# A token-mixing and attention kernel: heads laid out on partition mod 32, bonus added ahead of the output transposes, one replicated v for a batch; GpSimd adds the pair term, queues reordered

## The reference, cut to what matters

```python
def step(s, rkvw):                      # s: (b, h, i, j), one state of 16x16 per head
    r_t, k_t, v_t, w_t = rkvw
    a = k_t[..., :, None] * v_t[..., None, :]
    out = jnp.einsum('bhi,bhij->bhj', r_t, u * a + s)
    s = a + w_t[..., :, None] * s
    return (s, out)
...
og = out.reshape(b, l, h, s_)
m = og.mean(-1, keepdims=True)
va = ((og - m) ** 2).mean(-1, keepdims=True)
og = ((og - m) / jnp.sqrt(va + 1e-05)).reshape(b, l, e) * gn_w + gn_b
x1 = x + og * g @ Wo.T
```

## Time and profile before

| | |
|---|---|
| median of 3 runs | 1774.38 us (1774.17 to 1774.59) |
| the profiled execution | 1773.87 us, span 1772.1 us, granted TensorE clock 0.991 |
| busy: TensorE / VectorE | 1728.8 us (98%) / 1636.2 us (92%) |
| busy: ScalarE / GpSimd | 1180.4 us (67%) / 935.7 us (53%) |
| DMA | 180.8 MB, 102 GB/s over the span |

### The profile page before, as it was taken

The page is one execution under the profiler, slowest core; times in us unless marked ns, Lnnn a source line. Parts: engine busy times, 40 slices in busy tenths (PEclk is TensorE's granted clock), DMA queues, the critical chain, the costliest instruction groups (busy, mean ns, idle before and its releaser), DMA issues.

```text
span 1772.1 us, 33090 instructions
## 1 busy us (share of the span) xinstructions
PE 1728.8 (98%) x11570; PEld 1234.0 (70%) x11570; DVE 1636.2 (92%) x2224; ACT 1180.4 (67%) x2952; POOL 935.7 (53%) x752
## 2 busy tenths in 40 slices
PE   8899999999999999999999999999999999999878
PEld 6667667677767677767767766767776777776646
DVE  3699999999999999999999999999999999999993
ACT  4665677676667676667767667767666777666543
POOL 1344556555655654655655555665465565555540
PEclk9999999999999999999999999999999999999989
DMA  6343343343333344334344433334333334433420
GB/s 257 82 102 105 93 105 94 99 120 97 100 103 99 91 114 106 104 91 104 93 104 115 102 92 107 94 95 120 100 99 101 98 94 110 101 93 94 104 84 13
DMA packets 81732, 180.82 MB, mean 102 GB/s; under 512 B 18304, under 2 KB 35072, under 8 KB 80544
## 3 DMA queue, kind: packets, MB, share of 16 engines
q1 hardware_dynamic: 59920, 161.93, 35.0%
q10 hardware_dynamic: 21648, 16.78, 3.1%
HBM read 161.91 MB, written 16.78 MB: 101 GB/s over the span
## 4 chain that ended last, share of the span: by engine, by line
PE 84%; DVE 10%; issue 3%; ACT 1%; POOL 1%; DMA 0%; SPq 0%; DVEq 0%; POOLq 0%; ACTq 0%
PE bank L2014 29%; PE bank L2021 17%; PE bank L2138 6%; PE bank L2059 5%; PE bank L2046 5%; PE bank L2026 5%; PE bank L2095 4%; PE bank L2033 3%; DVE S L873 2%; PE bank L2074 2%; DVE A L855 2%; DVE A L885 2%; PE bank L2116 1%; PE bank L2149 1%; PE bank L2039 1%
## 5 line engine op out<-in xcount | busy, mean ns | idle before, releaser
L855 DVE TENSOR_TENSOR A<-vrep,kt 128x1008 f32<-128x1008 f32 x256 | 311.3, 1225 | 2.5
L560 POOL COPY S<-s 128x16 f32<-128x16 f32 x128 | 81.7, 639 | 419.0 <-DVE A L885 418.8
L873 DVE TENSOR_TENSOR_SCAN S<-wrep,S 128x512 f32<-128x512 f32 x256 | 299.7, 1212 | 1.2 <-issue 0.2
L885 DVE TENSOR_TENSOR A<-S,rt 128x2048 f32<-128x2048 f32 x128 | 292.0, 2282 | 0.1
L534 POOL TENSOR_TENSOR xf<-xf,xa 128x512 f32<-128x512 f32 x160 | 223.1, 1396 | 39.2 <-DVE xf L811 39.1
L1496 ACT ACTIVATE bank<-bank,par 128x128 f32<-128x128 f32 x640 | 173.4, 366 | 39.9 <-PE bank L2095 39.3
L503 POOL TENSOR_TENSOR hrs<-hrs,mhalf 128x32 f32<-128x32 f32 x31 | 171.0, 5517 | 2.6
L552 POOL TENSOR_TENSOR rk<-rT,kT 128x256 f32<-128x256 f32 x32 | 105.9, 3311 | 103.7 <-DVE oc L910 103.7
L501 POOL TENSOR_SCALAR rstd<-mv 128x1 f32<-128x1 f32 (+1 forms) x96 | 73.8, 769 | 156.9 <-DVE mv L748 61.4
L863 DVE TENSOR_TENSOR S<-A 128x1008 f32<-128x1008 f32 x128 | 155.5, 1215 | 0.2
L811 DVE TENSOR_TENSOR xf<-bank,sx 128x512 f32<-128x512 f32 x160 | 108.2, 677 | 44.7 <-PE bank L2014 22.7
(11 more groups left out here) (165 smaller groups left out, 4093.1 us busy)
## 6 DMA issues: line engine op xcount, KB each, us to landing
vrep<-v_dram SPq DMA_DIRECT2D x256, 512.0 KB
xc<-x_c SPq DMA_DIRECT2D x32, 256.0 KB, 6.5
xs<-x_s SPq DMA_DIRECT2D x32, 256.0 KB, 7.2
v_dram<-vT ACTq DMA_DIRECT2D x32, 256.0 KB, 3.1
out<-rr ACTq DMA_DIRECT2D x31, 256.0 KB, 2.7
st<-state SPq DMA_DIRECT2D x64, 2.0 KB, 6.4
Wv<-big_w SPq DMA_DIRECT2D x1, 1024.0 KB, 7.3
Wk<-big_w SPq DMA_DIRECT2D x1, 1024.0 KB, 9.0
```

Of the source, the lines that this page charges most:

```text
L855: ve_.tensor_tensor(A[:, u % 2, half * WJ:(half + 1) * WJ, 0:P - 2], vrep[:, half, :, 0:P - 2], k, ALU.mult).then_inc(dve_outer.sem, 1)
L873: last = ve_.tensor_tensor_scan(s, w, s, 0.0, ALU.mult, ALU.add)
L885: ve_.tensor_tensor(out4, s, r, ALU.mult).then_inc(dve_read.sem, 1)
```

## The change

What lies on a partition changes for v, k, r, the decay, u and the initial state: channel i of head h, which was 16h + i, goes to chunk i mod 4 and partition 32 (i div 4) + h, that is, each chunk holds four of the 16 channels of all 32 heads, with the head on partition mod 32. The weights and parameters are permuted accordingly before the launch.

```diff
+    by_value = np.arange(E).reshape(H, HS // C, C).transpose(2, 1, 0).reshape(E)
+    u = a["L1_u"].reshape(E)[by_value]
...
+        "big_w": np.stack([chunked(a["L1_" + k].T[:, by_value] if k in ("Wv", "Wk", "Wr") else a["L1_" + k].T) for k in BIG]),
```

```diff
-            def load_vrep(n, p, v):
-
-                src = v_dram[p].rearrange("(c h j) t -> c h (j t)", c=C, h=HC)
-                u, half = v // 2, v % 2
+            def load_vrep(n, p, half):
+
+                src = v_dram[p].rearrange("(h j) t -> h (j t)", h=H)
                 v0 = held(sp, regs[0], 16 * (n + 1))
-                v1 = held(sp, regs[1], dve_outer.count(f"a{(v - 2) % V}", n if v >= 2 else n - 1))
+                v1 = held(sp, regs[1], dve_outer.count(f"a{V - 2 + half}", n - 1))
...
-                             src[u][:, half * WJ * P:(half + 1) * WJ * P].unsqueeze(1).broadcast_to([HC, HS, WJ * P]))\
-                    .then_inc(vrep_loaded[half], 16)
+                             src[:, half * WJ * P:(half + 1) * WJ * P].unsqueeze(0).broadcast_to([C, H, WJ * P])).then_inc(vrep_loaded[half], 16)
...
-                eng.dma_start(v_dram[p].rearrange("(c e) t -> e c t", c=C), vT[:, p, :, :]).then_inc(v_stored, 16)
+                eng.dma_start(v_dram[p].rearrange("(h g c) t -> g h (c t)", h=H, c=C), vT[:, p, :, :].rearrange("e c t -> e (c t)")).then_inc(v_stored, 16)
...
-                    eng.wait_ge(act_tail.sem, act_tail.count("o4", n - 1))
-                ones = slide[:, HC * (3 - u):HC * (7 - u)]
+                    eng.wait_ge(dve_sum.sem, dve_sum.count("o4", n - 1))
+                ones = head_rep[:, 0:H]
                 for g in range(4):
-                    last = pe.matmul(bank[SUM_BANK][32 * g:32 * g + 32, :], ones, A[:, u % 2, g:UJ:4, :],
+                    last = pe.matmul(bank[SUM_BANK][32 * g:32 * g + 32, :], ones, A[:, u % 2, C * g:C * g + C, :],
```

```diff
+                eng.wait_ge(pe_bonus.sem, pe_bonus.count("C", n - 1))
+                for c in range(C):
+                    sc.activation(rkc[:, c, 0:P], bank_of("Rp")[:, c * P:(c + 1) * P], ACT.Copy, scale=col("u", c))
                 sc.activation(rT[:, :, :], by_chunk(bank_of("Rp")[:, :]), ACT.Copy)
...
-                eng.wait_ge(pe_tail.sem, pe_tail.count("C", n - 1))
-                po.tensor_tensor(rku[:, :, :], rT[:, :, :], kT[:, :, :], ALU.mult).then_inc(pool_wkv.sem, 1)
+                po.tensor_tensor(rkc[:, :, 0:P], rkc[:, :, 0:P], kT[:, :, :], ALU.mult).then_inc(pool_wkv.sem, 1)
...
+            def wkv_rks(n, m, p):
+
+                eng.wait_ge(pool_wkv.sem, pool_wkv.count("rk", n))
+                eng.wait_ge(pool_rk2.sem, pool_rk2.count("rk2", n))
+                po.tensor_tensor(rkc[:, 0:2, :], rkc[:, 0:2, :], rkc[:, 2:4, :], ALU.add).then_inc(pool_rks.sem, 1)
+                eng.wait_ge(pool_rks.sem, pool_rks.count("half", n))
+                po.tensor_tensor(rkc[:, 0, :], rkc[:, 0, :], rkc[:, 1, :], ALU.add).then_inc(pool_rks.sem, 1)
...
-                for c in range(C):
-                    last = pe.matmul(bank_of("C")[:, c * P:(c + 1) * P], head_u[:, c, :], rku[:, c, :],
-                                     start=True, stop=True)
-                last.then_inc(pe_tail.sem, 1)
...
-                pe.matmul(bank_of("C2")[:, 0:C * T2], head_rep[:, :], rk2[:, :, :].rearrange("p c m -> p (c m)"),
-                          start=True, stop=True).then_inc(pe_tail.sem, 1)
+                pe.matmul(bank_of("C")[:, 0:P + T2], head_rep[:, :], rkc[:, 0, :], start=True, stop=True).then_inc(pe_bonus.sem, 1)
```

```diff
+            def tail_ob(n, m, p):
+
+                eng.wait_ge(dve_bonus.sem, dve_bonus.count("o2", n))
+                b2 = second(by_chunk(oc[:, :]))
+                po.tensor_tensor(b2, b2, pv[:, :, :], ALU.add).then_inc(pool_bonus.sem, 1)
...
+            def tail_o4(n, m, p):
+                eng.wait_ge(pe_wkv.sem, pe_wkv.count(f"r{U - 1}", n))
+                eng.wait_ge(pe_tail.sem, pe_tail.count("Tx2", n - 1))
+                eng.wait_ge(pool_bonus.sem, pool_bonus.count("ob", n))
+                ve_.tensor_tensor(o4, by_chunk(bank[SUM_BANK][:, :]), by_chunk(oc[:, :]), ALU.add).then_inc(dve_sum.sem, 1)
...
-                o = bank[O_BANK][:, :].rearrange("t (c h k g) -> t k g c h", c=C, h=HC, k=4)
-                for k in range(4):
-                    pe.matmul(o[:, k], o4[:, k, :], ident[:, :], start=(k == 0), stop=False, is_transpose=True)
-                eng.wait_ge(dve_tail.sem, dve_tail.count("ob", n))
-                for c in range(C):
-                    last = pe.matmul(bank[O_BANK][:, c * P:(c + 1) * P], bonus[:, c * P:(c + 1) * P], ident[:, :],
-                                     start=False, stop=(c == C - 1), is_transpose=True)
+                o = bank[O_BANK][:, :].rearrange("t (h g k) -> t k g h", g=4, k=C)
+                for k in range(C):
+                    last = pe.transpose(o[:, k], o4[:, k, :], ident[:, :])
```

More of the change, by code:

```diff
@@ L108, in build @@
         head_rep = sb("head_rep", [P, P])
-        head_u = sb("head_u", [P, C, P])
-        slide = sb("slide", [P, 7 * HC])
         mhalf = sb("mhalf", [P, H])
@@ L199, in build @@
         Mn, Mm = probT[:, 2, :], probT[:, 3, :]
-        bonus = oc
         o4 = by_chunk(sq[:, :])
@@ L848, in wkv_outer @@
                 u, half = v // 2, v % 2
-                eng.wait_ge(vrep_loaded[half], 16 * (n * U + u + 1))
+                eng.wait_ge(vrep_loaded[half], 16 * (n + 1))
                 if v == 0:
@@ L1125, in opening @@
-                tail_mix(*at(0), 0)
+                wkv_outer(*at(1), 7)
+                wkv_read(*at(1), 2)
+                tail_rstd(*at(0))
+                wkv_pair(*at(1), 3)
                 att_rstd1(*at(3))
                 att_stats(*at(4))
+                att_aggr(*at(4))
+                mid_kw(*at(2))
+                wkv_scan(*at(1), 3)
                 wkv_read(*at(1), 3)
-                att_aggr(*at(4))
+                mid_gate(*at(2))
+                mid_shift(*at(3))
+                mid_xx(*at(3))
@@ L1189, in step @@
+                wkv_read(*b3, 3)
+                att_stats(*b0)
+                tail_mix(*b4, 0)
+                att_aggr(*b0)
+                mid_rw(*b2)
                 wkv_outer(*b2, 0)
-                wkv_read(*b3, 3)
+                tail_o4(*b3)
+                mid_shift(*b1)
+                att_rstd(*b0)
+                mid_xx(*b1)
                 wkv_outer(*b2, 1)
-                tail_mix(*b4, 0)
-                att_rstd1(*b1)
-                att_stats(*b0)
-                att_aggr(*b0)
@@ L1557, in mid_th @@
                 sc.activation(gT[:, p, :, :], by_chunk(bank_of("G")[:, :]), ACT.Tanh, scale=0.5).then_inc(act_mid.sem, 1)
-            def tail_o4(n, m, p):
-                eng.wait_ge(pe_wkv.sem, pe_wkv.count(f"r{U - 1}", n))
-                eng.wait_ge(pe_tail.sem, pe_tail.count("Tx2", n - 1))
-                sc.activation(o4, by_chunk(bank[SUM_BANK][:, :]), ACT.Copy).then_inc(act_tail.sem, 1)
             def tail_sq(n, m, p):
@@ L1769, in opening @@
+                mid_dt(*at(2))
+                mid_k(*at(2))
+                mid_ez(*at(2))
                 tail_xhat(*at(0))
+                mid_w(*at(2))
+                att_xhat(*at(3))
+                mid_th(*at(2))
+                mid_r(*at(2))
+                mid_xa(*at(3))
                 tail_xc2(*at(0), 0)
                 tail_xc2(*at(0), 1)
-                mid_r(*at(2))
-                mid_th(*at(2))
-                att_xhat(*at(3))
+                decay(*at(2), 0)
+                mid_tx(*at(3))
@@ L1818, in opening @@
                 tail_xc2(*at(1), 0)
+                fin_store(*at(0))
+                att_xhat(*at(4))
+                mid_r(*at(3))
+                mid_xa(*at(4))
+                tail_xc2(*at(1), 1)
             def step(on):
                 b0, b1, b2, b3, b4 = on
-                tail_xc2(*b4, 1)
                 decay(*b2, 0)
-                att_xhat(*b1)
-                mid_r(*b2)
+                mid_tx(*b1)
+                att_norm(*b0, 0)
+                att_norm(*b0, 1)
+                att_v(*b0)
@@ L1826, in step @@
+                mid_txt(*b1)
+                att_proj(*b0, 0)
+                att_proj(*b0, 1)
+                mid_bias(*b1, "w")
                 decay(*b2, 1)
-                att_v(*b0)
+                mid_bias(*b1, "v")
+                tail_sq(*b3)
+                att_exp(*b0, 0)
+                decay(*b2, 2)
                 fin_kr(*b4)
-                mid_th(*b2)
-                mid_xa(*b1)
-                tail_o4(*b3)
-                att_norm(*b0, 0)
+                att_exp(*b0, 1)
```

1264 lines of the change are left out of this document (592 added, 672 removed).

## The result

The changed kernel takes 1866.53 us (median of 4 runs, 1860.59 to 1869.32), the kernel before 1774.28 us in the same measurement: ratio 1.0517, 95% interval 1.0491 to 1.0543. It is slower by 92 us. The forecast was 1745 us, range 1735 to 1764: wrong in sign and far outside the range. The profiled execution took 1869.32 us with a span of 1867.5.

A forecast was written before the change was run, and what follows sets the result against it. TensorE was taken to bound the loop, needing 51.28 us and with misfits 51.5 instead of 52.52 a step; 26 steps save 26.5 us, edges 3: 1773.87 - 26.5 - 3 = 1744.4, median 0.5 above, 1745 us, range 1735 to 1764.

The forecast's parts named there:

- What bounds the kernel: In the loop of 26 steps, TensorE sets the 52.52 us step, with VectorE only 2 us behind.
- TensorE's bill: TensorE per step: 1.76 us removed, 0.32 added for one bonus matmul, 0.20 for tile-shape changes, leaving 51.28 us.
- VectorE's bill: VectorE per step: net +0.27 us of work, -0.36 from pulling dependent pairs apart, leaving 50.7 us.
- The collisions: GpSimd and VectorE on the shared port: new operations cost VectorE at most 1.99 us a step; 0.2 taken.
- the walk through the new queues: Rk product, first mix addition and sums over c fall on mixes, maxima and variance, supporting 0.2 us a step.
- Rival (c): Shared port: pair addition and sums over c hold VectorE off, 52.9 us a step, about 1781 us; chance 6%.
- DMA and SP: Loads and SP's queue: six of eight vrep loads a step go, no product waits for a load; worth 0.
- The cover of "18 to 21 us": VectorE's queue between the issue of the two remaining vrep loads and their use: 18 to 21 us.
- ScalarE and the tight place ahead of W1: ScalarE's xa, then VectorE's shift and xx, ahead of TensorE's W1: 0.3 us of room, 0.2 added for misfits.
- a wait of about 1 us for xa: At VectorE's shift: about 1 us waiting for ScalarE, replacing waits for scores and mix banks.
- The edges: Outside the steady loop, where pipeline fills and drains: -8 to +5 us possible, -3 taken.

The follow-up runs named there:

- the kernel with the placed products: Old-queue kernel (1815.61 us) with ScalarE's u scalings behind the gate's tanh and GpSimd's key product waiting for VectorE's fourth outer product: 1799.27 us.
- the run with small operations: Changed kernel with vrep loads moved ahead and split, GpSimd's mix additions, rk product, sums over c, pair and residual additions cut to about 8 columns: 1771.0 us.
- cutting the old additions: Changed kernel with vrep loads moved ahead and split (1818.7 us), GpSimd's five mix additions and residual addition cut to 8 columns: 1782.27 us.
- cutting the new operations: Changed kernel with vrep loads moved ahead and split (1818.7 us), only GpSimd's sums over c and pair addition cut to 4 or 8 columns: 1801.33 us.
- the kernel with both vrep edits: Changed kernel with both vrep loads ahead of s0 and x on SP's queue, each cut into four loads of 32 partitions: 1818.71 us.
- the old order: Changed kernel with vrep loads moved ahead and split, its engine queues in the order of the kernel before, new operations placed by hand: 1815.61 us.
- the best of these kernels: Old-queue kernel with placed scalings and key product (1799.27 us), plus GpSimd's pair product held to the scan's end and ScalarE's second normalisation earlier: 1796.24 us.
- with the operations cut small: Old-queue kernel (1815.61 us) with all GpSimd operations with two inputs cut to about 8 columns: 1781.25 us.

## Why the prediction was wrong

**What bounds the kernel: right before, wrong after.** TensorE's step, with VectorE 2 us behind, is what the rows show. That is also why the miss is so large: VectorE, forecast at 50.7, had no room for another 3 us. With the loads out of the way it is VectorE that sets the step, at 53.8.

**TensorE's bill: right in kind, 0.4 too low.** One bonus matmul costs 0.32 us (637.84 to 638.16 in the kernel with the placed products), as taken, and four transposes have gone. In the run with small operations TensorE is busy 494.01/500 x 52.27 = 51.64 us per step, predicted 51.28. About 0.1 of it is a slower start after its wait (W1 takes 1.19 us from start to start, 1.09 before); the rest was not traced.

**VectorE's bill: right.** 50.7 was forecast as the step less VectorE's waits, with 0.4 of collisions in it. With small operations the step of 52.27 less 1.0 of waits is 51.3, with 1.0 of collisions in it: 50.3 without them in both.

**The collisions: the term that failed.** The step read: "so they are 0.61 + 0.92 + 0.46 = 1.99 us", "at most 1.99 us a step", "I take 0.2". Two errors. The bound priced the new operations alone, where the change gives every old one a new neighbour as well: cutting the old additions gained 36 us, cutting the new operations 17. The true bound was all of GpSimd's two-tile work, some 10 us a step by the prediction's own count, not 1.99. And the walk through the new queues named only the rk product, the first mix addition and the sums over c. Four of the five that stretched VectorE in the step shown (the residual addition, a later mix addition, rk2, ez) were not among them, and the fifth, the sum over c, was walked wrongly: it met a product (+0.77), not a maximum. Measured: 3.8 us in the step shown, 3.6 in the kernel with both vrep edits, where cutting most of them gave 48 us. Rival (c) named this mechanism for the new operations, with a threshold of 1.8 us (1.6 by its own formula), and had 6%. With the 3.6 us of collisions that add up in one step of the kernel with both vrep edits, that formula gives 50.7 - 0.4 + 3.6 + 0.2 = 54.1 us, and 53.8 was measured there. The Trainium skill's rule ("SBUF — State Buffer", Who interferes with whom), that the one who issues first holds the shared pair for the whole instruction, agrees: maxima and other reductions and the reads of banks were never stretched (0.65 to 0.69 us for 512 columns in the whole trace after), products, pair sums and xx were, and a pair sum was held off 1.07 us by a 512-column addition.

**DMA and SP: worth 0, in fact 44 to 48 us.** Two sentences failed. "The two that stay are issued once the last products of the batch before have been made": the loads wait for that, but they stand on a queue behind s0 and x, whose waits end later (612.28 and 615.66 against 601.5 and 609.9). And "the x, state and s0 loads move earlier, past fewer vrep waits" looked at what these loads win, never at what the vrep loads lose. The cover of "18 to 21 us" was right for the product's distance in a queue that starts on time, not for this start. And the transfer itself was taken as before, though its shape changed: its outermost dimension is 4 where it was 8, and its landing takes some 13 us behind the loads ahead of it. The Trainium skill has the rule ("DMA: Bandwidth & Descriptors", Why a DMA increments its semaphore by 16 and not by 1): a copy is spread over as many DMA engines, up to 16, as divide the slowest dimension of both sides. By it the load runs on four. The trace agrees: 0.27 of the engines' time, 0.43 before, and cut into loads of 32 partitions each part lands in 2.8 us. The prediction did not apply this rule.

**ScalarE and the tight place ahead of W1: the right place, for another reason.** It was named with 0.3 us of room and priced at 0.2. In the kernel with small operations TensorE waits there 0.66 us a step. This and TensorE's 51.64 make 52.3, the period measured. But it is not ScalarE that is late: VectorE's shift, where a wait of about 1 us for xa was forecast, follows without one. VectorE, GpSimd and TensorE in that kernel, then VectorE's nmr in the kernel before:

```profile
650.03 0.80 DVE L721 SCALAR_TENSOR_TENSOR nmr<-mv,rstd 128x2 f32<-128x2 f32 x1
650.75 1.13 DVE L788 SCALAR_TENSOR_TENSOR xhat<-sx,par,xa 128x128 f32<-128x128 f32 x4
...
649.48 1.33 POOL L508 TENSOR_TENSOR rkc<-rT,kT 128x256 f32<-128x256 f32 x1
...
651.93 1.35 PE L2048 MATMUL bank<-w,xhat 128*128 128x160 f32 x8 [0.66 <-DVE xhat L788]
```

```profile
335.52 0.15 DVE L737 SCALAR_TENSOR_TENSOR nmr<-mv,rstd 128x2 f32<-128x2 f32 x1
```

rk2, which this run left whole, holds nmr off for 0.65 us, xx stands right behind nmr, and W1 waits for xx. So the one large collision that is left stands in the tight place and is as long as the wait.

**The edges: -3 forecast, +12 measured** in the kernel after, of which the third xin shows 6; no run traced the rest.

With the loads mended and most collisions cut, 1771 us are left, not 1745: 26 x (52.27 - 51.5) = 20 of the 26 us between lie in the loop. 26 x 0.63 = 16 of them would go, to about 1755 us, if the step fell to TensorE's 51.64 once rk2 left nmr alone. That is an estimate from these rows; no run tried it.

**What stays open.** Whether some order of the queues makes the new layout faster than before. In the old order, with some 1.1 us of collisions a step in the best of these kernels, 52.8 us remain, and as many with the operations cut small; three waits were removed one by one and each time another took its place, so that the loop between VectorE and TensorE, and not one wait, seems to hold it. That is argued from the waits and not shown. Some 15 us outside the steady steps of those kernels were not tried either. Nor did a run separate order and layout at the edges.

## What to carry to other kernels

When a change reorders queues, price the collisions of all work that gets a new neighbour, not of the new work: lay the two-tile operations of VectorE and GpSimd side by side for the whole step. For a load that moves, ask what stands ahead of it on its queue and when those waits end, and how its new shape spreads over the DMA engines; a load may need neither waits nor bytes of its own to be late. And where two engines are within 4% of each other, taking out one wait shows the next: until a run shows it, count on a small part of a wait (here 0.2 of 1.2 us).

## What was not expected of the hardware

GpSimd's waiting operation takes the port in the smallest gap. It went in among four VectorE operations that stand back to back (2.74 us in place of 1.14), and between two scans issued together (2.95 in place of 2.33). In return a two-tile operation of GpSimd that asks while a 2.28 us read of VectorE runs gets the port when the read ends: 3.25 us in its record, of which 2 are waiting, and VectorE lost nothing, since reductions followed. So a GpSimd operation can be aimed: a wait on the VectorE instruction ahead of a long read puts it beside what comes after the read.

Very small operations collide too. nmr, two columns, takes 0.15 us alone and 0.44 to 0.80 beside a GpSimd product: in the step shown both end at 571.3, so it pays the rest of the other's length, whatever its own. Such a row is easily passed over, and here it stood in front of the operation that TensorE waits for.

The load of 512 KB with an outermost dimension of four landed some 13.5 us after its issue, with another such load and both x loads issued just ahead; the same bytes as four loads of 32 partitions landed in 2.8 us each (2.3 to 5.2), at 0.42 us of SP's time per load.
